# Counting a sorted edge list in 25 spans of 50 destinations, one product per edge tile

## The reference

```
hv  = h.reshape(n, 12, 64);  ft = einsum('nhd,od->nho', hv, W)
e   = leaky_relu(a1[src] + a2[dst], 0.2)          # 20000 edges, sorted by dst
w   = exp(e - segment_max(e, dst)[dst])
alpha = w / max(segment_sum(w, dst)[dst], 1e-16)
agg = segment_sum(alpha[:, :, None] * ft[src], dst)
out = relu(agg + hv @ W_res.T)
```

## Time and profile before

| What | Value |
|---|---|
| Median of 3 runs | 1987.79 us (1981.37 to 1990.49) |
| Span of the profiled execution, first to last instruction | 1980.7 us |
| Mean granted TensorE clock over the span | 0.969 of full speed |
| PE busy over the span | 93% |
| DVE, ACT, POOL busy over the span | 38%, 20%, 7% |
| First one-hot to first weighting (the counting stage) | 376.12 to 524.10 us |

### The profile page before, as it was taken

The page is one execution under the profiler, slowest core; times in us unless marked ns, Lnnn a source line. Parts: engine busy times, 40 slices in busy tenths (PEclk is TensorE's granted clock), DMA queues, the critical chain, the costliest instruction groups (busy, mean ns, idle before and its releaser), DMA issues.

```text
span 1980.7 us, 24631 instructions
## 1 busy us (share of the span) xinstructions
PE 1841.1 (93%) x8438; PEld 1157.9 (58%) x8439; DVE 746.3 (38%) x1757; ACT 403.9 (20%) x1065; POOL 131.6 (7%) x170
## 2 busy tenths in 40 slices
PE   7999999999899999599997999999999999699895
PEld 4555566567533334366666965555579579455563
DVE  3212222497788989511114401151111124522121
ACT  2341210024312222111002422000221211212121
POOL 0000000000000000111114100000000000022221
PEclk9999999999999999699998999999999999799898
DMA  6003100000000101545555211010010013546575
GB/s 186 0 1 133 38 0 1 21 0 1 21 31 31 49 25 42 199 144 189 185 189 159 77 48 47 2 48 0 1 48 1 0 63 94 206 106 155 160 183 133
DMA packets 53756, 149.59 MB, mean 76 GB/s; under 512 B 9394, under 2 KB 20038, under 8 KB 53157
## 3 DMA queue, kind: packets, MB, share of 16 engines
q1 hardware_dynamic: 34101, 88.97, 13.0%
q0 software_dynamic: 12032, 37.59, 7.8%
q10 hardware_dynamic: 7536, 21.85, 3.1%
HBM read 117.92 MB, written 37.83 MB: 79 GB/s over the span
## 4 chain that ended last, share of the span: by engine, by line
PE 82%; DVE 8%; DMA 4%; issue 2%; DVEq 2%; ACT 1%; POOL 0%; ACTq 0%; SPq 0%; POOLq 0%
PE PS L691 24%; PE PS L1020 10%; PE PS L701 8%; PE PS L840 5%; PE PS L1130 5%; PE PS L1150 4%; PE PS L762 4%; PE PS L1102 4%; DVE WRA L1779 3%; PE PS L1088 3%; PE PS L1061 3%; PE PS L929 2%; DMA WS<-in_fW 2%; PE PS L938 2%; DVE WRB L1779 2%
## 5 line engine op out<-in xcount | busy, mean ns | idle before, releaser
L691 PE MATMUL PS<-WS,XT 128*125 128x384 f32 x960 | 313.8, 489 | 1.4 <-issue 1.4
L691 PEld LDWEIGHTS PS<-WS,XT 128*125 128x125 f32 x960 | 180.6, 189 | 129.7 <-issue 3.9
L1020 PE MATMUL PS<-WS,XGT 128*128 x600 | 199.5, 490 | 0.0
L1020 PEld LDWEIGHTS PS<-WS,XGT 128*128 128x128 f32 x600 | 113.1, 192 | 74.5 <-issue 2.2
L701 PE MATMUL PS<-XT,WS 128*128 128x416 f32 (+1 forms) x432 | 151.2, 512 | 0.0
L1779 DVE SCALAR_TENSOR_TENSOR WRA<-RB,U,AT 125x500 f32<-125x500 f32 (+1 forms) x240 | 140.0, 647 | 8.5 <-ACT AT L1255 6.6
L1913 DVE TENSOR_TENSOR YS<-PS,EBB 128x768 f32<-128x768 f32 x48 | 46.0, 958 | 245.6 <-PE PS L1020 191.2
L701 PEld LDWEIGHTS PS<-XT,WS 128*128 128x128 f32 x432 | 81.6, 189 | 69.2 <-issue 69.2
L1130 PE MATMUL PS<-WS,XGT 128*128 x288 | 105.0, 518 | 11.6 <-DMA WS<-in_fW 10.5
L929 PE MATMUL PS<-WRA,F 125*64 125x500 f32 (+1 forms) x480 | 100.0, 535 | 10.0 <-DVE WRA L1779 9.5
L584 POOL DMA_INDIRECT XG<-xn_rows,IDX x53 | 52.1, 982 | 761.7 <-DVEq L1874 642.1
(11 more groups left out here) (313 smaller groups left out, 2234.8 us busy)
## 6 DMA issues: line engine op xcount, KB each, us to landing
WS<-in_ewT SPq DMA_DIRECT2D x8, 2304.0 KB, 10.4
WS<-in_fW SPq DMA_DIRECT2D x16, 1152.0 KB, 8.3
WS<-in_w SPq DMA_DIRECT2D x5, 2304.0 KB, 9.5
expert_rows<-YS ACTq DMA_DIRECT2D x25, 384.0 KB
xn_rows<-XN ACTq DMA_DIRECT2D x20, 336.0 KB
RB<-expert_rows SPq DMA_DIRECT2D x12, 488.3 KB
WS<-in_wp SPq DMA_DIRECT2D x2, 2304.0 KB
WS<-in_W SPq DMA_DIRECT2D x2, 2304.0 KB, 8.2
```

The costliest lines, as they stand in the source:

```text
L691: last = nc.tensor.matmul(ps[0:T, 0:HC], lhsT[:, k, t * T:(t + 1) * T], w[:, k, b * HC:(b + 1) * HC], start=(k == 0), stop=(k == KC - 1))
L1020: last = nc.tensor.matmul(PS[:, 4 + 2 * a + b, 0:HC], XGT[:, a, k, :], WS[:, bass.ds(slot, 1), k * C + b * HC:k * C + (b + 1) * HC].rearra ...
```

## The change

- **Spans.** 25 spans (`NW`) of 50 destinations (`WD`) in place of ten of 125. A turn is 3 tiles in place of 6, and there are 3 slots in place of 6.
- **One-hots.** A source is split as `s = 125 * block + rest`. Per tile DVE makes `OHS` (125 edges x 128, `rest`) and `OHK` (125 edges x 500: 50 destinations x 10 blocks). For this the second column of `ES` becomes `dst * 10 + block`, made once by five more small operations near 36 us (rounding by adding and taking off `MAGIC`). `OHK` is one `tensor_scalar` with two operations: subtract the column, then compare with `-500 * w`.
- **Product.** One matmul per tile, `OHS` as weights and `OHK` as the 500 moving columns, into one bank; four banks alternate (`WB`).
- **Layout.** The bank holds `rest` on the partitions and (destination, block) along them: already `AT`'s layout. One ACT instruction per span copies it, with the two free axes exchanged, straight into `AT`. `AROW`, its copies and the 100 transposes are gone.
- **`ft` rounds.** Two before each of the spans 0, 2, ..., 18.
- **Waits and constants.** PE waits for the copy of the span four before; DVE waits for all 25 copies before the weighting. The iota of 500 is made at the kernel's start, so the iota of 1250 and its cast at the stage's start are gone. The DMA of the third unit's rows no longer waits for the stage. The number of turns in the table is rounded in place of counted.

```diff
-SLOTS = 6
+MAGIC = float(3 << 22)
+WD = 50
+NW = N // WD
+KW = WD * NT
+WB = 4
+SLOTS = 3
...
+FT_AT = {2 * t: t for t in range(NT)}
...
@@ sync @@
-            if u == 2:
-                sp.wait_ge(tr_emptied, len(TRR))
...
@@ gpsimd @@
-        pool.wait_ge(pe_filled, J.filled(J.at[f"proj0_{NT - 1}"] + 1))
-        nc.gpsimd.iota(iota_i, pattern=[[1, N]], base=0, channel_multiplier=0).then_inc(consts, 1)
+        nc.gpsimd.iota(iok_i, pattern=[[1, KW]], base=0, channel_multiplier=0).then_inc(consts, 1)
...
@@ tensor @@
-        for g in range(NT):
-            n = nc.tensor.value_load(table[0:1, 1, g:g + 1], min_val=2, max_val=TURNS)
-            done_before = nc.tensor.value_load(table[0:1, 2, g:g + 1], min_val=0, max_val=TURNS * NT)
+        for w in range(NW):
+            n = nc.tensor.value_load(table[0:1, 1, w:w + 1], min_val=2, max_val=TURNS)
+            done_before = nc.tensor.value_load(table[0:1, 2, w:w + 1], min_val=0, max_val=TURNS * NW)
+            ps = PS[:, w % WB, 0:KW]
             def counted(u, first):
                 for k in range(SLOTS):
                     pe.wait_ge(oh_ready, u * (2 * SLOTS) + 2 * k + 2)
-                    for c, (o, w) in enumerate(CH):
-                        last = nc.tensor.matmul(PS[0:T, 3 * (g % 2) + c, 0:w], OHD[:, k, :], OHS[k][:, o:o + w],
-                                                start=(first and k == 0), stop=True, skip_group_check=True)
-                    last.then_inc(oh_free, 1)
...
+                    nc.tensor.matmul(ps, OHS[:, k, :], OHK[:, k, :], start=(first and k == 0), stop=True,
+                                     skip_group_check=True).then_inc(oh_free, 1)
+            if w in FT_AT:
+                for q in range(2):
+                    turn_round(2 * FT_AT[w] + q)
+            if w >= WB:
+                pe.wait_ge(at_ready, w - WB + 1)
...
-            if g >= 1:
-                for q in range(3):
-                    turn_round(round_of["at", g - 1, q])
...
@@ scalar @@
-            for c, (o, n) in enumerate(CH):
-                nc.scalar.activation(AROW[:, g % 2, o:o + n], PS[0:T, 3 * (g % 2) + c, 0:n], ACT.Copy).then_inc(arow_ready, 1)
...
+            act.wait_ge(acc_done, w + 1)
+            nc.scalar.activation(AT[:, :, w * WD:(w + 1) * WD], PS[0:T, w % WB, 0:KW].rearrange("p (d s) -> p s d", s=NT),
+                                 ACT.Copy).then_inc(at_ready, 1)
...
@@ vector @@
-        dve.wait_ge(consts, 9)
         V.memset(zeros, 0.0)
-        V.tensor_copy(iota, iota_i)
         V.drain().then_inc(iota_done, 1)
...
                 for k in range(SLOTS):
                     dve.wait_ge(oh_free, u * SLOTS + k + 1)
-                    V.tensor_scalar(OHD[:, k, :], iota[0:T, g * T:(g + 1) * T], ES[:, 1, bass.ds(tile + k, 1)],
-                                    None, ALU.is_equal).then_inc(oh_ready, 1)
-                    V.tensor_scalar(OHS[k], iota[0:T, :], ES[:, 0, bass.ds(tile + k, 1)],
-                                    None, ALU.is_equal).then_inc(oh_ready, 1)
+                    V.tensor_scalar(OHS[:, k, :], io128, ES[:, 0, bass.ds(tile + k, 1)], None,
+                                    ALU.is_equal).then_inc(oh_ready, 1)
+                    V.tensor_scalar(OHK[:, k, :], iok, ES[:, 1, bass.ds(tile + k, 1)], -float(KW * w), ALU.subtract,
+                                    ALU.is_equal).then_inc(oh_ready, 1)
+        dve.wait_ge(at_ready, NW)
         dve.wait_ge(tr_emptied, len(TRR))
```

More of the change, by code:

```diff
@@ L250, in graph_transformer @@
     LR = {1: sb("LR1", [P, 2, T])}
[L251 to L256, removed]
-    WBD = sb("WBD", [P, 2 * P])
-    gidx = sb("gidx", [80, 2, NT])
-    gidx_i = sb("gidx_i", [80, 2, NT], I32)
+    assert cursor[0] <= top - XNB * C * 4 - 8192 - 4512, cursor[0]
+    cursor[0] = top - XNB * C * 4 - 8192 - 4512
+    WBD = sb("WBD", [P, 2 * P])
+    attn_sb = sb("attn_sb", [D, 2 * H])
+    vv = sb("vv", [P, 2 * H])
+    iok = sb("iok", [T, KW], F16)
+    gidx = sb("gidx", [80, 2, NW])
+    gidx_i = sb("gidx_i", [80, 2, NW], I32)
     tidx = sb("tidx", [80, 2])
@@ L262, in graph_transformer @@
     mnx = sb("mnx", [80, 2, 2])
[L263 to L267, removed]
+    hit = sb("hit", [80, 2, 2, NW])
+    rng = sb("rng", [2 * NW, 1])
+    span = sb("span", [1, 8, NW])
+    table = sb("table", [1, 3, NW], I32)
     assert cursor[0] <= top - XNB * C * 4 - 8192
@@ L422, in graph_transformer @@
     R_ROWS = -(-H * N // C)
[L423 to L428, removed]
+    TRR = [(t, q) for t in range(NT) for q in range(2)]
     assert R_ROWS * C <= 2 * N // P * P * C
@@ L850, in _ @@
                 counted(done_before + j, False)
-            nc.tensor.matmul(PS[0:T, 3 * (g % 2) + 2, 0:16], zeros[:, 0:T], zeros[:, 0:16], start=False, stop=True,
+            nc.tensor.matmul(ps[:, 0:16], zeros, zeros[:, 0:16], start=False, stop=True,
                              skip_group_check=True).then_inc(acc_done, 1)
-            if g >= 1:
-                for q in range(3):
-                    turn_round(round_of["at", g - 1, q])
-        for q in range(3):
-            turn_round(round_of["at", NT - 1, q])
         pe.wait_ge(tr_emptied, len(TRR))
@@ L1725, in _ @@
                 tile = nc.s_assert_within(t0 + j * SLOTS, 0, ETP - SLOTS, skip_runtime_bounds_check_because=
-                                          "a span's first tile is at most ETP less the tiles of its turns")
+                                          "a window's first tile is at most ETP less the tiles of its turns")
                 for k in range(SLOTS):
                     dve.wait_ge(oh_free, u * SLOTS + k + 1)
-                    V.tensor_scalar(OHD[:, k, :], iota[0:T, g * T:(g + 1) * T], ES[:, 1, bass.ds(tile + k, 1)],
-                                    None, ALU.is_equal).then_inc(oh_ready, 1)
-                    V.tensor_scalar(OHS[k], iota[0:T, :], ES[:, 0, bass.ds(tile + k, 1)],
-                                    None, ALU.is_equal).then_inc(oh_ready, 1)
+                    V.tensor_scalar(OHS[:, k, :], io128, ES[:, 0, bass.ds(tile + k, 1)], None,
[3 more added lines that the diff above has]
+        dve.wait_ge(at_ready, NW)
         dve.wait_ge(tr_emptied, len(TRR))
```

113 lines of the change are left out of this document (47 added, 66 removed).

## The result

| What | Before | After |
|---|---|---|
| Median of the runs of the comparison | 1986.79 us (1980.72 to 1995.70, 9 runs) | 2001.18 us (1990.01 to 2007.41, 9 runs) |
| Ratio after / before, 95% interval | | 1.0066 [1.0038, 1.0094] |
| Span of the profiled execution | 1980.7 us | 1999.4 us |
| Mean granted TensorE clock over the span | 0.969 | 0.94 |
| First one-hot to first weighting | 147.98 us | 163.61 us |

The changed kernel is slower by 0.4 to 0.9%, about 14 us; the forecast was 2004. The profiled execution itself took 2001.18 us, so 1.8 us lie around its span.

A forecast was written before the change was run, and what follows sets the result against it. PE was taken as the bound, with DVE late next after the change. +0.4 us at full clock and 16 for the low clock gave +16.4 on the 1980.7 us span: 1997, median 2004; 8-in-10 range 1985 to 2024.

The forecast's parts named there:

- The start: Before the counting stage's first one-hot: POOL's iota wait and most of the cast go, first one-hot 1.3 us earlier.
- The changes of span: On DVE's sequencer: branch and three table reads cost 2.52 us at each of 24 changes, 60.5 us.
- The rival in which the reads hide: DVE's sequencer gets ahead at span changes and its reads hide; wholly hidden -49 us, 1939; chance 0.07.
- The tiles: DVE's 182 tiles that follow another in their span: 0.48 us each, with 0.46 and 0.58 as ends.
- the slot loop of 0.46 a tile: Three slots tie a tile to PE's end three tiles earlier: 1.375 us at full clock, 1.73 at half.
- The two-operation one-hot: DVE's 500-wide one-hot lasts 0.35 us, with no penalty for two operations on 2-byte data.
- The end of 0.6 ns an element: Rival: the two-operation one-hot on DVE is slower, 0.17 us more a tile; +30 us, 2018; chance 0.07.
- The clock: TensorE at 1.2 GHz for about half the stage: 16 us of a possible 32.5.
- The first term: Slots at the low clock: 182 x (0.576 - 0.48) = 17.5 us if all low, half of it expected.
- The second: PE's ft rounds at nine span changes: 15 us if all at low clock, half of it expected.
- the sum at full clock: Tiles, changes, start and end of the stage together, ft rounds costing nothing: +0.4 us with 0.48 a tile.
- The sum: Stage and kernel lengthen by +0.4 + 16 = +16.4 us; span 1997, median 2004.

The follow-up runs named there:

- e_two: Changed kernel with two table reads per span on DVE and one on PE, the turn count taken as a difference of registers; 1985.10 us, ratio 0.9984.
- e_read4: Changed kernel with one more table read on DVE at each span, four in place of three; 2012.35 us, ratio 1.0109.
- e_static: Changed kernel without table reads, loops and registers in the counting on DVE and PE, constants and written-out turns instead; 1932.22 us (one run).
- e_slots6: e_wd100 with 6 slots and turns of 6 tiles in place of 3; 1969.89 us, ratio 0.9890.
- e_warm2: Changed kernel with unread fp32 filler products on PE after spans' closing products, 1 before ft rounds, 3 elsewhere; 1989.38 us, ratio 0.9989.
- e_slots4: e_wd100 with 4 slots and turns of 4 tiles in place of 3; 1969.08 us, ratio 0.9881.
- e_reads: Changed kernel with one table read fewer per span on DVE and PE, turns done before summed in a register; 1992.78 us, ratio 1.0037.
- e_best: e_slots4 with the table of e_two, two reads on DVE and one on PE; 1957.37 us, ratio 0.9841 to the kernel before.
- e_warm: Changed kernel with unread fp32 filler products on PE after spans' closing products, 2 before ft rounds, 6 elsewhere; 2007.29 us, ratio 1.0121.
- e_wd100: Changed kernel with 13 spans of 100 destinations, one-hot of 1000 columns and two products of 500 per tile; 1972.91 us, ratio 0.9917.

## Why the prediction was right, step by step

**The start.** Forecast 1.3 us gained. From the last addition to the first one-hot it was 4.26 us before and 2.97 after: 1.29.

**The changes of span.** Forecast 24 x 2.52 = 60.5, measured 60.4: 2.47 for a usual one, and a few slower (2.58 to 2.90) that make up the rest, by luck. The mechanism was right: the reads and the branch run one after the other on DVE's sequencer, 0.57 to 0.63 us a read (e_two, e_read4), and they vanish with the registers (e_static). The reading behind the 2.52 was rough. In the kernel before, span 5's last small one-hot came at 474.77, not right after its slot was free at 474.10, and the first read started at 474.55, so the sequencer had a lead of 0.22; from that read to the next one-hot were 2.32 us, as good as the changed kernel's 2.30. The rival in which the reads hide was wrong for this kernel and right in its condition: it needs an engine slower than the sequencer and slots to run ahead in, and then they nearly hide (e_slots6). The kernel before had both between spans 0 and 1 and had lost most of the lead where slots were short. The Trainium skill (Advanced Engine Details and Errata, Sequencer Loop) has further engine instructions read and queued while control runs. The trace of e_slots6 agrees: its third read starts at 400.18, ahead of the span's last small one-hot at 400.46. But the lead is limited by the slots, and with three of them at 0.43 us a tile nothing is hidden.

**The tiles.** Forecast 182 x 0.48 = 87.4 at full clock. Measured, with 0.6 us for each of the nine turns behind `ft` rounds: 59.7 + 22.5 + 5.4 = 87.6. The prediction had two reasons for about this pace, and one of them holds. The 0.48 itself came from the sequencer, with a branch every third tile, and that is what the trace shows: in span 0 the sequencer's rows follow one another with no gap over 0.10 us, 1.40 us for a turn of three tiles, 0.47 each, where the engine alone needs 1.27 (e_static). Only its pieces were off, 0.35 us for a plain tile and the rest at the turn in place of 0.42 and 0.06. So within a turn tiles run at the engine's 0.425, and every third start has 0.13 us on top in span 0 and 0.16 to 0.2 in the later ones, at either clock (e_warm2), which goes when the loop goes (e_static). The other reason, the slot loop of 0.46 a tile, does not bind. Its sum put 0.05 + 0.18 us between the large one-hot's end and its product; the trace has 0.06 (397.61 + 0.34 to 398.01). With the product's 0.385 us the loop is 1.20 us for three tiles in place of 1.375, and with its 0.60 at the low clock 1.41 in place of 1.73, just under a turn.

**The two-operation one-hot.** Forecast 350 ns with no penalty, measured 344. The end of 0.6 ns an element was far off.

**The clock.** Forecast 16 us: half of 17.5 for slots at the low clock, and half of 15 for the `ft` rounds. The clock was lower than expected (0.69 in place of 0.75) and its cost 12.0 us (e_warm2). The first term failed, since it rested on the slot loop, whose 1.73 us were 1.41: tiles and turns take the same at either clock (82.2 us at the low, 81.8 in e_warm2). The second was too small: the rounds' waits took 19.2 - 5.4 = 13.8 us over a plain turn, 11.2 of them due to the clock. Eight of the nine pairs of rounds ran at the low clock (2.92 us long, the ninth 1.57), not half of them. The first term, 8.7, should have been nothing and the second, 7.5, should have been 11 to 12. Besides, the sum at full clock put the rounds at nothing, and e_warm2 shows 8.0 - 5.4 = 2.6. That the clock's two terms came out at 16 for 12, near enough, is partly luck.

The Trainium skill (TensorE: Matmul & The Clock Gate, HAM oscillation) tells of bursts with waits between them that fall back to the low clock again and again. The trace agrees: the granted clock of the stage is 0.69, which is the low level for some 60% of it.

**The sum.** Forecast for the stage's lengthening, from the last addition on: +16.4. Measured: 152.24 to 166.58, +14.3. The median of the runs rose by 14.4; the profiled spans differ by 18.7. The step from the span to the median, 7.1 us, is 5.3 us of scatter if the time around the span was 1.8 us as it is after: the profiled execution before was a fast one. The changed kernel's profiled execution stood at the median, so its span, forecast at 1997, was 1999.4 and the median 1.8 above that, not 7.1. So the 2004 has one error of 2.4 us down and one of 5.3 up in it.

## What to carry to other kernels

- Before cutting a loop into more and shorter pieces, count what its control costs: here each table read took 0.6 us on the sequencer and each turn's branch put 0.13 to 0.2 us between one-hots. The 24 changes took 60 us, while PE's busy time in the stage fell by 24. The trace shows this time as idle time released by "issue", and the sequencer's own rows say what it was.
- Control is free only while the sequencer is ahead. That takes an engine slower than the sequencer and enough slots; compare both per-tile times, and see whether the kernel before had a lead that the change takes away.
- Taking work off a busy PE can lower its clock. What then suffers is the dense piece on the path between two engines, not the sparse work itself.

## What the runs showed that had not been expected

**The last 290 us vary by steps.** The profiled execution of e_slots4 has a stage 20.3 us shorter than the kernel before, but a span only 9.3 us shorter. The chain of waits in its last layer (start, us, work):

```profile
1798.87 13.07 DMA WS<-in_fW
...
1823.41 13.52 DMA WS<-in_fW
...
1874.16 10.42 DMA WS<-in_fW
...
1893.49 13.79 DMA WS<-in_fW
```

The chain waits for a weight transfer four times here, three times in the profiled execution of the kernel before and of the changed one, twice in those of e_static, e_reads and e_best. Elsewhere (e_warm, e_warm2, e_wd100, e_two) three, in e_slots6 and e_read4 four. From the last product that reads `AT` to the end of the span it took 298 to 302 us in the three executions with four waits and 279 to 290 in the nine others. So two spans can differ by up to 23 us for what happens behind the stage, and the experiments were judged by the stage first. What decides the number was not tried.

**Some tiles are slow in the same place in every run.** In the changed kernel three tiles within a turn take 0.67, 0.80 and 0.73 us in place of 0.43 (in the first turns of its sixth, eleventh and last span). In e_warm and e_warm2 the same three do; in e_read4 one does, in e_reads four and in e_two two, all at other places; in e_static, without loops, none. The edges are the same in all of them, so it goes with the program's code and not with the data; its cause is open.

**A narrower weight load is not a shorter one.** The 207 weight loads of 125 rows x 128 columns in bf16 had a median of 103 ns (95 to 152), though the clock was low for most of the stage, and of 96 in e_warm2, where it was high. Those of 125 x 125 in the kernel before had one of 137 (132 to 229) at the high clock.
